# Splitting an expert kernel's weights into bf16 pairs ahead of time on GpSimd

## The reference

```python
x = x + xattn0(layernorm(x), ctx, Wq, Wkv, Wout)          # 16 heads, softmax
x = x + ffn0(layernorm(x), w_gate, w_up, w_down)          # fake-quantised SwiGLU
x = x + xattn1(layernorm(x), ctx, ctx, igate, fgate, ...) # mLSTM heads: 4, with decay
# layer 1 FFN: 8 experts, the top 2 of each token
probs = softmax(layernorm(x) @ gate_w); weights, idx = top_k(probs, 2)
weights = weights / weights.sum()
for i in range(8):
    wi = where(idx == i, weights, 0).sum(-1)
    h = silu(xn @ w1[i]) * (xn @ w3[i])                   # w1, w3: 256 x 1024
    out += (h @ w2[i]) * wi                               # w2: 1024 x 256
x = x + out
```

## Time and profile before

| | |
|---|---|
| time, median of 3 runs | 858.18 us (857.07 to 863.29) |
| time of the profiled execution | 865.73 us |
| its span, first to last instruction | 864.0 us |
| mean granted TensorE clock | 0.879 |
| busy: PE, DVE, ACT, POOL | 679.8, 527.0, 410.6, 278.8 us |

### The profile page before, as it was taken

How to read it: one execution, slowest core, us unless ns; L and a number is a source line. 1 busy time by engine, 2 the same in 40 slices (tenths; PEclk the granted TensorE clock), 3 DMA queues, 4 the chain that set the end, 5 groups by cost and what they waited for, 6 DMA issues and landing times.

```text
span 864.0 us, 19336 instructions
## 1 busy us (share of the span) xinstructions
PE 679.8 (79%) x4571; PEld 471.9 (55%) x4615; DVE 527.0 (61%) x1371; ACT 410.6 (48%) x831; POOL 278.8 (32%) x390
## 2 busy tenths in 40 slices
PE   2999999885853991577417989898989998989992
PEld 2788887663322670466404556565656555655661
DVE  5577789985867452788785464646454555464441
ACT  1466655556874463345225444545353545553430
POOL 3111111111436001644302263535354253553421
PEclk9799999986978795555558999999999999999996
DMA  8100000000000114211270514243331525431213
GB/s 260 32 13 12 16 14 13 0 1 1 0 0 12 44 42 159 87 28 27 97 245 19 169 30 132 67 128 73 105 90 31 170 34 165 124 73 24 34 22 110
DMA packets 45844, 58.41 MB, mean 68 GB/s; under 512 B 13497, under 2 KB 39417, under 8 KB 45273
## 3 DMA queue, kind: packets, MB, share of 16 engines
q1 hardware_dynamic: 38328, 47.79, 16.9%
q0 software_dynamic: 7488, 10.31, 7.2%
HBM read 145.90 MB, written 11.80 MB: 183 GB/s over the span
## 4 chain that ended last, share of the span: by engine, by line
PE 48%; DVE 18%; issue 14%; POOL 7%; DMA 3%; ACT 3%; DVEq 2%; POOLq 1%; ACTq 1%; SPq 0%
PE psum L995 16%; PE psum L1017 7%; PE psum L718 3%; PE psum L1008 3%; POOL region L658 3%; PE psum L702 3%; PE psum L725 3%; PE psum L895 2%; PE psum L738 1%; PE psum L757 1%; PE psum L707 1%; PE psum L840 1%; PE psum L888 1%; DVE region L1358 1%; DMA region<-xrow_dram,next_token 1%
## 5 line engine op out<-in xcount | busy, mean ns | idle before, releaser
L995 PE MATMUL psum<-region 128*128 x897 | 209.6, 382 | 19.8 <-POOL pause_p L660 6.2
L995 PEld LDWEIGHTS psum<-region 128*128 128x128 bf16 x936 | 91.6, 98 | 119.1 <-issue 30.4
L1017 PE MATMUL psum<-region 128*128 x936 | 112.5, 278 | 6.2 <-DVE region L1868 3.7
L1017 PEld LDWEIGHTS psum<-region 128*128 128x128 bf16 x936 | 91.3, 100 | 22.3 <-issue 9.2
L1261 ACT ACTIVATE region<-psum 128x512 f32<-128x512 f32 x78 | 46.5, 596 | 115.0 <-PE psum L995 104.2
L1838 DVE TENSOR_TENSOR region<-psum,region 128x512 f32<-128x512 f32 x78 | 53.9, 690 | 72.9 <-ACT region L1261 62.9
L628 POOL TENSOR_TENSOR pause_p<-minus_half 128x1 f32<-128x1 f32 x37 | 7.1, 193 | 191.4 <-DVE next_token L1854 190.6
L640 POOL DMA_INDIRECT sum_dram<-region,tok_idx x39 | 62.0, 1589 | 6.6 <-issue 6.3
L1282 ACT ACTIVATE pause_a<-one_col 128x1 f32<-128x1 f32 x117 | 23.7, 202 | 84.1 <-issue 70.2
L525 POOL TENSOR_TENSOR region<-region,pair_mask 128x256 f32<-128x256 f32 x32 | 18.9, 612 | 137.8 <-ACT region L1062 137.8
L1868 DVE TENSOR_TENSOR region<-psum,region 128x1024 bf16<-128x1024 f32 x39 | 47.6, 1222 | 20.1 <-ACT region L1269 20.1
(11 more groups left out here) (304 smaller groups left out, 1386.0 us busy)
## 6 DMA issues: line engine op xcount, KB each, us to landing
region<-in_L_ffn_w SPq DMA_DIRECT2D x117, 1024.0 KB
region<-in_ctx SPq DMA_DIRECT2D x48, 128.0 KB, 2.1
region<-neg_max_dram SPq DMA_DIRECT2D x4, 1024.0 KB, 7.6
xrow_dram<-region SPq DMA_DIRECT2D x1, 2080.0 KB, 7.8
x_sb<-in_x SPq DMA_DIRECT2D x4, 512.0 KB, 7.1
sum_dram<-x_sb SPq DMA_DIRECT2D x1, 2048.0 KB, 7.5
region<-in_L_ffn_w_down SPq DMA_DIRECT2D x1, 704.0 KB, 8.1
region<-in_L_ffn_w_gate SPq DMA_DIRECT2D x1, 640.0 KB, 8.6
```

Source lines behind the costliest of these rows:

```text
L995: last = mm(psum[:, 2 * f + n, :], (xT_lo if xl else xT_hi)[:, p, k, :], weights_at(place, wl, n, k * F1 + f * FH, FH), start=(i == 0), st ...
L1017: last = mm(psum[:, 7, 0:D], (hT_lo if hl else hT_hi)[:, f, :], weights_at(place, wl, 2, f * D, D), start=(i == 0), stop=(i == 3 * (F1 // ...
```

## The change

ScalarE and VectorE no longer split weights. POOL splits all 24 matrices once, in pieces of 512 columns (four casts, then four subtractions). SP loads each whole matrix and stores its pair in `split_dram`.

- Parts 0 to 13 (experts 2 to 6, without the last matrix of expert 6) are split in attention 1: part b-1 after the mask of batch b, in a ring of three buffers.
- Part 14 and the six matrices of experts 0 and 1 are split in front of attention 2, after POOL's memsets. The last six pairs are written straight to slots 0 and 1 of `expert_w`. SP stores part 14 and those of expert 1, and does this before it waits for the gates. The loads of `ctx_c` move from SP to ScalarE's queue.
- The three matrices of expert 7 are loaded when SP is at tile 2 and split one piece (cast and subtraction) per tile beside tiles 1 to 12, and stored when SP is at tile 15.
- In the tiles SP loads ready pairs, 1 MB each, two matrices for tile t when tile t-3 has its gate and up products, the third one step later; a load is skipped where the expert isn't new or is already in its slot.
- A layer norm statistics copy (L1388) becomes a reduction over one element, and `tile_info` is laid out by tile and has the slot first.

```diff
+            def load_part(i):
+                view, width = weight_part(i)
+                if i >= 2 and i != EARLY_PARTS and i < MIXED + FIRST_PARTS:
+                    sp.wait_ge(part_split, i - 1)
+                sp.dma_start(whole_part(i)[0]..., view).then_inc(part_loaded[ring_of(i)], 16)
+            def store_part(i):
+                sp.wait_ge(part_split, i + 1)
+                e, n = part_of(i)
+                sp.dma_start(split_dram[e, n, :, :], whole_part(i)[1]).then_inc(part_stored[ring_of(i)], 16)
...
-            with sp.Fori(0, B // 2 - 1) as i:
-                for p in range(2):
-                    sp.wait_ge(t1_done, 2 * i + p + 1)
-                    sp.dma_start(ctx_sb[:, p, :], ctx_in[2 * i + (p + 2), :, :]).then_inc(ctx_loaded[p], 16)
+            for b in range(B - 2):
+                sp.wait_ge(t1_done, b + 1)
+                sp.dma_start(ctx_sb[:, b % 2, :], ctx_in[b + 2, :, :]).then_inc(ctx_loaded[b % 2], 16)
+                if b >= 2:
+                    store_part(b - 2)
+                load_part(b)
+            for i in range(B - 4, EARLY_PARTS):
+                store_part(i)
             sp.wait_ge(x2_ready, B // 2)
             for b in range(2):
                 sp.dma_start(ctx_c[:, b, :], ctx_in[b, :, :]).then_inc(cctx_loaded[b], 16)
-            with sp.Fori(0, B // 2 - 1) as i:
-                for p in range(2):
-                    sp.wait_ge(ct_done, 2 * i + p + 1)
-                    sp.dma_start(ctx_c[:, p, :], ctx_in[2 * i + (p + 2), :, :]).then_inc(cctx_loaded[p], 16)
+            load_part(EARLY_PARTS)
+            load_part(EARLY_PARTS + 1)
+            for i in range(EARLY_PARTS, MIXED + FIRST_PARTS):
+                if part_of(i)[0] > 0:
+                    store_part(i)
+                if i + 2 < MIXED + FIRST_PARTS:
+                    load_part(i + 2)
             sp.wait_ge(gates_read, B)
...
+            for t in range(NT + 1):
+                if t < NT:
+                    info = info_of(t)
+                    if t >= 1:
+                        sp.wait_ge(gate_up_loaded, 32 * t)
+                    if t >= 3:
+                        sp.wait_ge(gu_done, 2 * t - 4)
+                    load_matrix(0, info, gate_up_loaded)
+                    load_matrix(1, info, gate_up_loaded)
+                if t >= 1:
+                    if t >= 2:
+                        sp.wait_ge(down_loaded, 16 * (t - 1))
+                    if t >= 4:
+                        sp.wait_ge(dn_done, t - 2)
+                    load_matrix(2, info_before, down_loaded)
...
+            PIECES = [slice(c, c + CHUNK) for c in range(0, PART, CHUNK)]
+            def high_piece(i, n):
+                whole, pair = whole_part(i)
+                nc.gpsimd.tensor_copy(pair[:, PIECES[n]], whole[:, PIECES[n]]).then_inc(part_high, 1)
+            def low_piece(i, n):
+                whole, pair = whole_part(i)
+                pool.wait_ge(part_high, len(PIECES) * i + n + 1)
+                last = nc.gpsimd.tensor_tensor(pair[:, PART:2 * PART][:, PIECES[n]], whole[:, PIECES[n]], pair[:, PIECES[n]], ALU.subtract)
+                if n == len(PIECES) - 1:
+                    last.then_inc(part_split, 1)
+            def split_part(i):
+                part_free(i)
+                for n in range(len(PIECES)):
+                    high_piece(i, n)
+                for n in range(len(PIECES)):
+                    low_piece(i, n)
...
-            mask_k(1, 1)
-            with pool.Fori(0, (B - 2) // 2) as i:
-                mask_k(2 * i + 2, 0, inner=True)
-                mask_k(2 * i + 3, 1, inner=True)
+            for b in range(1, B):
+                mask_k(b, b % 2)
+                if b - 1 < EARLY_PARTS:
+                    split_part(b - 1)
...
-            nc.gpsimd.memset(v_c, 1.0).then_inc(q_preset, 1)
+            nc.gpsimd.memset(v_c, 1.0).then_inc(v_preset, 1)
+            for i in range(EARLY_PARTS, MIXED + FIRST_PARTS):
+                split_part(i)
...
+                if t >= 1:
+                    i, n = pieces[t - 1]
+                    if n == 0:
+                        part_free(i)
+                    high_piece(i, n)
+                    low_piece(i, n)
...
+            def front_c(b, p, more=True):
                 act.wait_ge(ct_done, b + 1)
+                if more:
+                    act.dma_start(ctx_c[:, p, :], ctx_in[b + 2, :, :]).then_inc(cctx_loaded[p], 16)
...
-                nc.vector.tensor_copy(mv[:, b, :], mv1[:]).then_inc(chain, 1)
+                nc.vector.tensor_reduce(mv[:, b, :], mv1[:].unsqueeze(2), AX.X, ALU.max).then_inc(chain, 1)
...
+            link_d(tt(tneed, te, tcum, ALU.not_equal))
+            link_d(nc.vector.scalar_tensor_tensor(tneed, tcum, 1.5, tneed, ALU.is_ge, ALU.max))
+            link_d(tt(tneed, tneed, tchg, ALU.mult))
...
-            weights_low(0, 0, 0)
-
-            dve.wait_ge(ranks_done, 2)
+            dve.wait_ge(dn_done, 1)
```

More of the change, by code:

```diff
@@ L38, in build @@
     SLOT = 2 * 3 * PART
+    PARTS = 3 * E
+    EARLY_PARTS = 14
+    FIRST_PARTS = 6
+    LAST_PARTS = 3
+    MIXED = PARTS - LAST_PARTS - FIRST_PARTS
+    CHUNK = 512
+    OTHERS = (TOP - 1) * B
     H1 = ig_k.shape[1]
@@ L340, in build @@
         xg_loaded = [sem(f"xg_loaded{i}") for i in range(2)]
[L342 to L344 removed]
+        part_loaded = [sem(f"part_loaded{i}") for i in range(3)]
+        part_stored = [sem(f"part_stored{i}") for i in range(3)]
+        part_split = sem("part_split")
+        part_high = sem("part_high")
+        gate_up_loaded = sem("gate_up_loaded")
+        down_loaded = sem("down_loaded")
         tx_done = sem("tx_done")
@@ L451, in _ @@
             sp.dma_start(xrow_dram[0:B * P, :].rearrange("(b p) c -> p b c", p=P), xrow).then_inc(rows_stored, 16)
+            for r in range(3):
+                sp.wait_ge(part_stored[r], 16 * stores(r, MIXED + FIRST_PARTS))
+            sp.wait_ge(part_split, MIXED + FIRST_PARTS)
             sp.wait_ge(info_ready, 1)
[L454 to L464 removed]
@@ L482, in _, with info_of @@
-            load_step(0, 0)
-            with sp.Fori(0, (NT - 5) // 2) as i:
-                load_step(2 * i + 1, 1, inner=True)
-                load_step(2 * i + 2, 0, inner=True)
-            for t in range(NT - 4, NT):
-                load_step(t, t % 2)
+            def info_of(t):
+                slot = sp.value_load(tile_info[0:1, t, 0:1], min_val=0, max_val=(SLOTS - 1) * SLOT)
+                expert = sp.value_load(tile_info[0:1, t, 1:2], min_val=0, max_val=E - 1)
+                need = sp.value_load(tile_info[0:1, t, 2:3], min_val=0, max_val=1)
+                return slot, expert, need
@@ new lines, in load_matrix @@
+            def load_matrix(n, info, signal):
+                slot, expert, need = info
+                sp.dma_start(expert_w[:, bass.ds(slot + n * 2 * PART, 2 * PART)],
+                             split_dram.rearrange("e n p c -> p e n c")[:, bass.ds(expert, 1), n, :].rearrange("p e c -> p (e c)"),
+                             cond=(need > 0)).then_inc(signal, 16)
+            for t in range(NT + 1):
[13 more added lines that the diff above has]
+                    load_matrix(2, info_before, down_loaded)
+                info_before = info
+                if t == 2:
+                    for i in range(PARTS - LAST_PARTS, PARTS):
+                        load_part(i)
+                if t == OTHERS - 1:
+                    for i in range(PARTS - LAST_PARTS, PARTS):
+                        store_part(i)
+                    for r in range(3):
+                        sp.wait_ge(part_stored[r], 16 * stores(r, PARTS))
@@ L544, in _ @@
                 nc.gpsimd.tensor_tensor(rstd[:, part], rstd[:, part], minus_half[:, part], ALU.pow).then_inc(rstd2_ready, 1)
+            for r in range(3):
+                pool.wait_ge(part_stored[r], 16 * stores(r, EARLY_PARTS))
             def hidden_product(g, t):
@@ L665, in step_d @@
                     add_rows(t - 1, 1 - p, inner)
-                weights_low(t + 2, p, inner)
             pool.wait_ge(info_ready, 1)
-            for t in range(3):
+            pieces = [(i, n) for i in range(PARTS - LAST_PARTS, PARTS) for n in range(len(PIECES))]
+            for t in range(len(pieces) + 1):
                 step_d(t, t % 2)
-            with pool.Fori(1, (NT - 3) // 2) as i:
+                if t >= 1:
[4 more added lines that the diff above has]
+                    low_piece(i, n)
+            with pool.Fori(len(pieces) // 2, (NT - 3) // 2) as i:
                 step_d(2 * i + 1, 1, inner=True)
@@ L1526, in hidden @@
                         clip_group(t // 2 + 2)
+            for r in range(3):
+                dve.wait_ge(part_stored[r], 16 * stores(r, EARLY_PARTS))
             hidden(0, first=True)
```

167 lines of the change are left out of this document (65 added, 102 removed).

## The result

The changed kernel takes 871.03 us (median of 4 runs, 870.3 to 875.34) beside 857.62 for the kernel before: a ratio of 1.014, 95% interval 1.0113 to 1.0167. In a second group it took 875.05 beside 859.13, ratio 1.0182 (1.0149 to 1.0215). The profiled execution is 871.28 us, span 869.2, clock 0.878.

A forecast was written before the change was run, and what follows sets the result against it. TensorE was taken to bound the tiles, with gaps at expert changes from GpSimd's low half of w1. Terms -25.3 -1.5 +1.5 +19.5 +17 gave +11 on 858.2, so 869 us, range 847 to 890.

The forecast's parts named there:

- Tiles, -25.3 -1.5 +1.5: Expert tiles: L658's stalls go, -25.3 us; VectorE's lighter work at the front, -1.5; loading changed experts and expert 7, +1.5.
- A split, 7.7 us: GpSimd's price for one split: four casts at 0.66 and four subtractions at 1.27 us, between 7.4 and 8.0.
- In front of attention 2, +19.5: Seven splits delay SP's last store and so the gate exchange by 17.0 us, plus 2.5 queued behind that store.
- The cover of the projections: In front of attention 2: projections have up to 20 us of cover, so slower loads and ScalarE's issuing cost nothing.
- Attention 1, +17: Attention 1: late first mask, norms held by GpSimd's splits and delayed weight preparation cost 17 us, between +5 and +40.
- (a): Start of attention 1: the first split makes the mask of batch 2 late, +2.9 us once (0 to 5).
- (c): Attention 1: 13 VectorE norms each wait about 0.7 us for a GpSimd piece, +9 us (0 to 23).
- (d): Late steps of attention 1: VectorE's weight preparation collides with splits 11 to 13, +5 us.
- Rival 1: Attention 1 and gate stage: VectorE slips between GpSimd's pieces and the terms cancel; -5, 853 us, chance 0.28.
- Rival 2: Before attention 2: a split under 6.3 us nearly removes the gate delay; -14, 844 us, chance 0.08.
- Rival 3: Attention 1: GpSimd's queue starves VectorE, norms wait for the split's end (23 us); +34, 892 us, chance 0.13.
- Rival 4: Expert tiles: late bulk loads keep TensorE waiting at expert changes, so no gain; +36, 894 us, chance 0.05.

The follow-up runs named there:

- e6: Changed kernel with ScalarE issuing the gate exchange, each early split one mask later and expert 7's loads at tile 4; 863.09 us, ratio 1.0051.
- e3: Changed kernel with the seven splits in front of attention 2 replaced by a memset of zeros each; 865.15 us, ratio 1.0007.
- e7: Changed kernel with parts 3 to 13 unsplit and the seven splits before attention 2 replaced by memsets; 858.56 us, ratio 0.9997.
- e10: e6 with the first ten splits in one piece, all others in four, and the last store after the maxima's loads; 858.71 us, ratio 0.994.
- e2: Changed kernel with ScalarE instead of SP issuing the gate exchange, after its last projections; 869.34 us, ratio 1.0057.
- e1: Changed kernel with parts 3 to 13 loaded and stored but not split; 866.82 us, ratio 1.0026.
- e5: Changed kernel with the early splits in pieces of 256 columns, eight casts and eight subtractions; 876.93 us, ratio 1.0158.
- e8: e6 with all splits ahead of the tiles in one piece and the last store after the maxima's loads; 869.41 us, ratio 1.0071.

## Why the prediction was right

The forecast was 869 us (847 to 890), the result 871.03. The total came out near, and that is in part luck: the tiles were 8 us too favourable, the terms in front of attention 2 6.5 us too dear and attention 1 2.4 us. The three large terms had their sign and main mechanism right. TensorE's clock was missing, and the sizes of a split, of the held norms and of the loads' effects were wrong.

- **Tiles, -25.3 -1.5 +1.5.** Measured -19.4 in the tiles and +2.6 ahead of them: too favourable by 8 us. L658's stalls are all gone. Tiles 2 to 38 gained 19.5 for 23.8, since 36 steps average 9.42 us where a clean one is 9.24 (I took 9.19). The term ahead of them had the wrong sign. Expert 7's three loads start at 469.95, 4 us ahead of the first gather, which then takes 6.06 us to land where it took 3.06; e6, which moves them, gets 3.3 us back (its gather lands after 3.05), and 2.2 more in the tiles. In my term ahead of the tiles these loads stood at nothing.
- **A split, 7.7 us.** 6.78. The subtraction went by the row of 1.27 us and took 1.13 alone; the cast took 0.57 for 0.66. The rule of the Trainium skill (GPSIMD Engine Reference, section 3.1) had led to about 7 us, nearer than my row. Its estimate of 0.44 us for the loop of a cast lies under the 0.57 measured for the whole cast.
- **In front of attention 2, +19.5.** +10.6 and +2.4. The mechanism was right: SP's last store waits for the last split, and the exchange goes out right behind it (344.25, 344.27, 344.67). The size of the 17.0 was wrong. The seven splits took 47.7 us with all that they met, where I had 57.2 (53.9 and 3.3 for norms): the pieces are shorter, and a norm hardly lengthens one (6.7 to 7.0 us a split, 6.78 alone). Against that GpSimd waits 3.6 us for 1 MB loads, which my sum did not have. The exchange behind 1 MB cost 2.4 for my 2.5 (gone in e3, e7 and e10).
- **The cover of the projections.** I gave them "up to 20 us". They end 6.9 us later than before, counted from the first norm, and the exchange goes out 10.5 us later. So they were covered in the changed kernel, as I had it, with 3.6 us to spare. But "costs nothing" holds only while SP is later still: e2 takes SP away and gains 3.0 us up to the exchange. In the kernel before and in e2, e3 and e7 the exchange follows the last copy of gates within 0.05 us. What makes the projections late in the changed kernel is by TensorE's rows 4.0 us of waits for contexts, and 3.4 us at 1.2 GHz from 309.1 on, behind the longest of these waits (306.2 to 308.7); held norms show there as no wait of TensorE.
- **Attention 1, +17.** +14.6. (a) The late mask, +2.9: the two steps around it took 5.6 and 8.2 us longer, of which 2.4 and 3.3 are the wait. The rest goes with the clock at 1.2 GHz, which my sum put at nothing. (c) The norms, +9: seven plain-step norms are held for 0.25 to 0.5 us each, and those steps are 0.19 us longer, 1.3 in all. I had 13 norms and 0.7 each; the others run outside the splits, but for the one of 3.10 us. (d) The preparation, +5: 3.2, 3.4 and 1.2 us, 7.8 in all, in which the clock falls for 3.4 us twice (162.4 and 176.0) in the first profile. Ahead of the late mask both profiles are 1 to 1.5 us shorter than before. e1 confirms the division: without splits 3 to 13 the last scores come 7 to 9 us sooner (e1 and e7 against the profile with the same time at the lower clock: 8.2 and 8.9), and (c) and (d) are 9.1.
- **Carrying the difference of 0.9%** between profiled execution and median over to the forecast was not right. The changed kernel's profiled execution lies on its median (871.28 and 871.03), 6 us under the 877 that I had for it; the 8 us of before were that one execution's (the second lay 2.5 us under the median of its group). As a difference of medians the change is +13.4 and +15.9 where I had +11. By the stages of two profiles each it is +9.2.
- **Rival 1** (VectorE slips between the pieces) is refuted for attention 1 by e5, where the norm of each plain step waited for the end of the run, and holds in front of attention 2: there the norms of the changed kernel end at piece boundaries (one ran 302.24 to 303.29 with a run of 301.98 to 306.65). **Rival 2** needed a split under 6.3 us; it took 6.78. **Rival 3** has the right mechanism for attention 1, but its price of 23 us assumed that each norm meets a whole split; it meets the last 0.3 to 0.5 us. **Rival 4** is refuted: the tiles gained 19.4.
- The exclusive port of the Trainium skill (SBUF — State Buffer, section "Who interferes with whom") agrees in two points: operations that read PSUM are untouched (0.69 us in e8), and a held norm ends with an instruction of GpSimd. That it would wait for one piece only does not agree with 49.10 to 52.20, nor with e5. Nor did the 1539 ns that I said agreed: that norm began in the first memset and sat through its end.

What stays open: why a norm sits through piece boundaries in the plain steps of attention 1, while norms in front of attention 2 and operations of the weight preparation get in at one; no run here changes only that. That the late mask brings the clock down is read from seven profiles in which TensorE waited 1.25 to 3.33 us for it and the clock fell, and seven with 0.89 us or no wait, in which it did not; no run changes the wait alone. The 4.6 us that stay in e3 are put down to the transfers by the context waits (3.3 us there), not by a run without transfers. And the medians of after and before differ by 4 to 7 us more than the stage lengths do.

## What to carry to other kernels

Work moved to an idle engine is paid where operations of another engine are held by it, so cost it by phase: where the other engine's operation falls in the step, and whether the moved work is over by then. Where it can be over in time, take the largest pieces, since they finish first (6.0 us for 6.8, and the norms of attention 1 untouched). Where operations meet it anyway, take small ones: norms of 0.6 us for 1.2 in front of attention 2, and last five steps of attention 1 of 65.3, 63.1 and 61.8 us with one, four and eight pieces.

A wait of TensorE can cost more than its length: 2.4 us of it were followed by 6.8 us at half the clock, and the two steps took 5.6 us longer. So look at the granted clock behind each new wait before you put the time down to something else.

Ask of every "cover" how much of it is used: here the projections used 6.9 of 10.5 us, so that taking away what covered them gave only the rest. And bulk loads cost through the small loads that they delay.

## What the hardware showed beyond expectation

- A TENSOR_SCALAR of 128x256 with two per-partition scalars, 0.40 us alone, took up to 4.30 us beside GpSimd subtractions; held norms end about 0.15 us after the run (plain steps of attention 1) or after a piece (in front of attention 2), in every one that I read. The reductions and subtractions on PSUM kept their 1.22 us beside the same pieces, and the reductions of x_sb their 0.74 for two.
- TensorE's granted clock fell to 1.2 GHz for 6.8 or 10.2 us in each of the seven profiles in which it had waited 1.25 to 3.33 us for the mask of batch 2; the two steps around it took 3.2 to 4.9 us more than the wait explains. A wait of 3.41 us for a context in e7 (from 311.5) was followed by no fall.
- On GpSimd 2048 columns cost 1.89 + 4.08 us in one piece, 2.28 + 4.50 in four, 2.81 + 5.08 in eight.
- Two bulk transfers back to back on SP's queue (1 MB store, 1 MB load) landed after 8.15 us, where the first of two loads with no store ahead took 5.54; a 64 KB load 0.5 us behind a 1 MB store took 5.3 us.
- The kernel before differed by 0.8% between groups, which ran on different chips (857.6 to 864.7); whether it is the chip or the time is not shown. The changed kernel ran in two groups and had ratios of 1.014 and 1.0182. A ratio from one group is not to be set beside one from another at this size.
